# Softmax attention on one core: the maxima products read every fourth query as strided weights

## The reference

```python
B, S, D = 2, 2048, 256          # the input is (2, 2048, 256)
H, DH = 16, 64
q = (c_q @ w_up_q.T).reshape(b, s, H, DH).transpose(0, 2, 1, 3)
k = (c_kv @ w_up_k.T).reshape(b, s, H, DH).transpose(0, 2, 1, 3)
v = (c_kv @ w_up_v.T).reshape(b, s, H, DH).transpose(0, 2, 1, 3)
q = _apply_rope_subspace(q, DR)
k = _apply_rope_subspace(k, DR)
scale = 1.0 / np.sqrt(DH)
scores = jnp.einsum('bhqd,bhkd->bhqk', q, k) * scale
attn = jax.nn.softmax(scores, axis=-1)
out = jnp.einsum('bhqk,bhkd->bhqd', attn, v)
out = out.transpose(0, 2, 1, 3).reshape(b, s, H * DH)
out = out @ w_out.T + residual
```

## Time and profile before

| | us |
|---|---|
| median of 3 runs | 4254.92 (4253.44 to 4257.21) |
| profiled execution | 4258.81 |
| its span, first to last instruction | 4257.0 |
| TensorE, matmuls busy | 3884.0 (91%) |
| TensorE, weight loads busy | 2962.6 (70%) |
| VectorE busy | 3592.9 (84%) |
| ScalarE busy | 2636.8 (62%) |
| GpSimd busy | 2218.4 (52%) |
| granted TensorE clock, mean | 0.952 |

### The profile page before, as it was taken

How to read it: one execution, slowest core, us unless ns; L and a number is a source line. 1 busy time by engine, 2 the same in 40 slices (tenths; PEclk the granted TensorE clock), 3 DMA queues, 4 the chain that set the end, 5 groups by cost and what they waited for, 6 DMA issues and landing times. The chain is left out here.

```text
span 4257.0 us, 54965 instructions
## 1 busy us (share of the span) xinstructions
PE 3884.0 (91%) x17786; PEld 2962.6 (70%) x17786; DVE 3592.9 (84%) x4513; ACT 2636.8 (62%) x3523; POOL 2218.4 (52%) x1841
## 2 busy tenths in 40 slices
PE   7959978869999999999999999999999999989563
PEld 4635535548888888888888888888888888867421
DVE  7845558869999999999999999999999999946521
ACT  6724334347777777777777777777777777732221
POOL 2547756745555555555555555555555555520155
PEclk9969989989999999999999999999999999989676
DMA  7223446842232222332222322224222232046295
GB/s 267 53 60 61 67 105 241 271 128 54 52 77 59 57 56 50 69 69 55 57 51 60 79 53 61 52 52 84 52 59 54 52 74 62 17 152 220 64 250 111
DMA packets 323409, 379.73 MB, mean 89 GB/s; under 512 B 141388, under 2 KB 250769, under 8 KB 310067
## 3 DMA queue, kind: packets, MB, share of 16 engines
q1 hardware_dynamic: 298486, 345.70, 32.2%
q0 software_dynamic: 24640, 30.52, 4.2%
HBM read 232.47 MB, written 117.79 MB: 82 GB/s over the span
## 5 line engine op out<-in xcount | busy, mean ns | idle before, releaser
L1592 POOL TENSOR_TENSOR at_pl<-at_pf,at_ph 128x512 fp32r<-128x512 f32 x1024 | 1328.8, 1298 | 1314.0 <-ACT at_ph L1739 1313.9
L1738 ACT ACTIVATE at_pf<-at_ps_s 128x1024 f32<-128x1024 f32 x1024 | 1051.5, 1027 | 728.2 <-PE at_ps_s L1791 728.2
L1655 DVE TENSOR_TENSOR at_pl<-at_pf,at_ph 128x512 fp32r<-128x512 f32 x1024 | 1349.3, 1318 | 22.3 <-ACT at_ph L1739 22.3
L1637 DVE TENSOR_REDUCE at_mx<-at_ps_u 128x2 f32<-128x1024 f32 x1016 | 1240.1, 1221 | 12.8 <-PE at_ps_u L1775 9.2
L1739 ACT ACTIVATE at_ph<-at_ps_s 128x1024 fp32r<-128x1024 f32 x1024 | 1044.6, 1020 | 0.0
L1807 PE MATMUL at_ps_v<-at_ph,at_vh 128*128 128x512 f32 x2048 | 810.7, 396 | 0.2 <-POOL at_pl L1592 0.2
L1809 PE MATMUL at_ps_v<-at_pl,at_vh 128*128 128x512 f32 x2048 | 808.9, 395 | 0.0
L1808 PE MATMUL at_ps_v<-at_ph,at_vl 128*128 128x512 f32 x2048 | 806.9, 394 | 0.0
L1808 PEld LDWEIGHTS at_ps_v<-at_ph,at_vl 128*128 128x128 f32 x2048 | 388.2, 190 | 91.5
L1807 PEld LDWEIGHTS at_ps_v<-at_ph,at_vh 128*128 128x128 f32 x2048 | 387.4, 189 | 92.3 <-POOL at_pl L1592 0.6
L1809 PEld LDWEIGHTS at_ps_v<-at_pl,at_vh 128*128 128x128 f32 x2048 | 384.9, 188 | 90.2
(11 more groups left out here) (274 smaller groups left out, 4910.3 us busy)
## 6 DMA issues: line engine op xcount, KB each, us to landing
wgu<-Wgu_in SPq DMA_DIRECT2D x64, 384.0 KB, 5.1
qT<-pj_rot SPq DMA_DIRECT2D x32, 512.0 KB, 5.5
vT<-pj_vo SPq DMA_DIRECT2D x16, 1024.0 KB, 5.8
kT<-pj_rot SPq DMA_DIRECT2D x32, 512.0 KB, 3.1
k<-kT SPq DMA_DIRECT2D x32, 512.0 KB, 10.4
q<-qT SPq DMA_DIRECT2D x32, 512.0 KB, 9.4
at_q<-at_low SPq DMA_DIRECT2D x128, 128.0 KB, 2.3
at_vf<-vT SPq DMA_DIRECT2D x32, 512.0 KB, 8.6
```

What stands on the lines that cost most here:

```text
L1592: pool.tensor_tensor(pl[:, n % NP, at], pf[:, n % NP, at], ph[:, n % NP, at].bitcast(F32), ALU.subtract).then_inc(s["pl2_ready"], 1)
L1637: dve.tensor_reduce(mx[:, qb % 2, 2 * i:2 * i + 2], maxima_at(base, j)[:, 0:2], X, ALU.max).then_inc(s["u_max"], 1)
L1655: dve.tensor_tensor(pl[:, n % NP, at], pf[:, n % NP, at], ph[:, n % NP, at].bitcast(F32), ALU.subtract)\
L1738: act.activation(pf[:, n % NP], ps_s[:, n % 2], ACT.Exp, scale=DH ** -0.5)
```

## The change

The tile `qp`, the semaphore `qp_ready`, the function `gather_queries` with its calls and the wait of `products` are removed. The weights of a maxima product are read from `q1` itself, with a step of four elements (16 bytes) between the 128 columns. Both matmuls of a product read them so. Nothing else is changed.

```diff
--- before.py
+++ after.py
@@ -1423,7 +1423,6 @@
             k2 = [self.k2_0, sb("k2_1", [P, L], F32R)]
             q1 = [self.q1_0, sb("q1_1", [P, L], F32R)]
             q2 = [sb(f"q2_{i}", [P, L], F32R) for i in range(2)]
-            qp = sb("qp", [P, L], F32R)
             raw = [self.raw0, sb("raw_1", [P, L], F32R)]
             cut = sb("cut", [P, 2, QB], U32)
             low = sb("low", [P, 2, QB], F32R)
@@ -1445,7 +1444,7 @@
             ps_s = ps("ps_s", [P, 2, 2 * QB])
             ps_v = ps("ps_v", [P, 2, QB])
             ps_u = ps("ps_u", [P, 2, QB])
-            names = ("turns raw0 raw1 kq0 kq1 v0 v1 fixed own cut_ready low_ready low0 low1 qp_ready u_full u_max mg_ready nm_ready "
+            names = ("turns raw0 raw1 kq0 kq1 v0 v1 fixed own cut_ready low_ready low0 low1 u_full u_max mg_ready nm_ready "
                      "row0 row1 row2 row3 s_full p_ready pl_ready pl2_ready vh_ready v_split pv_done "
                      "o_ready o0_out o1_out den recip rden").split()
             s = {n: sem(n) for n in names}
@@ -1720,35 +1719,19 @@
                     act.wait_ge(s[f"o{qb % 2}_out"], g * 64 + (32 * (qb // 2) + 32))
                     act.activation(o_st[:, qb % 2], ps_v[0:DH + 1, qb % 2], ACT.Copy).then_inc(s["o_ready"], 1)
 
-                def gather_queries(g, hh, half, qb):
-
-                    if qb == 0:
-                        loaded(act, "kq", hh, half, 64)
-                    if not isinstance(g, int) or g > 0:
-                        act.wait_ge(s["u_full"], g * SLOTS + ((qb + 1) * PER - SLOTS))
-                    at = slice(qb * QB, (qb + 1) * QB)
-                    act.activation(qp[:, at].rearrange("d (t p) -> d t p", t=NQB),
-                                   q1[hh][:, at].bitcast(F32).rearrange("d (p t) -> d t p", t=NQB), ACT.Copy)\
-                        .then_inc(s["qp_ready"], 1)
-
-                def pair(pr, last=False):
+                def pair(pr):
                     for n in range(2 * SLOTS):
                         act.wait_ge(s["s_full"], pr * (2 * SLOTS) + (n + 1))
                         act.wait_ge(s["pv_done"], pr * (2 * SLOTS) + (n + 1))
                         act.activation(pf[:, n % NP], ps_s[:, n % 2], ACT.Exp, scale=DH ** -0.5)
                         act.activation(ph[:, n % NP], ps_s[:, n % 2], ACT.Exp, scale=DH ** -0.5)\
                             .then_inc(s["p_ready"], 1)
-                        if n % PER == PER - 2 and not (last and n >= SLOTS):
-                            hh, qb = n // SLOTS, n % SLOTS // PER
-                            gather_queries(pr * 2 + (hh + 1), 1 - hh, pr + hh, qb)
                         if n % PER == 2 and n > PER:
                             output(pr * 2 + (n - PER) // SLOTS, (n - PER) % SLOTS // PER)
                         elif n == 2 and pr > 0:
                             output(pr * 2 - 1, NQB - 1)
-                for qb in range(NQB):
-                    gather_queries(0, 0, 0, qb)
                 for pr in range(PAIRS):
-                    pair(pr, pr == PAIRS - 1)
+                    pair(pr)
                 output(HEADS - 1, NQB - 1)
 
             @block.tensor
@@ -1767,9 +1750,7 @@
                             pe.wait_ge(s["u_max"], j - 2)
                     else:
                         pe.wait_ge(s["u_max"], base * SLOTS + j)
-                    if i == 0:
-                        pe.wait_ge(s["qp_ready"], base * NQB + qb + 1)
-                    tile = qp[:, qb * QB + i // 2 * P:qb * QB + (i // 2 + 1) * P]
+                    tile = q1[hh][:, qb * QB:(qb + 1) * QB].rearrange("d (p t) -> d t p", t=NQB)[:, i // 2]
                     for w in range(2):
                         kb = i % 2 * 2 + w
                         m = pe.matmul(maxima_at(base, j)[:, w], tile, k1[hh][:, kb * QB:(kb + 1) * QB],
```

## The result

| | before | changed |
|---|---|---|
| median, us | 4257.52 (6 runs, 4253.44 to 4265.77) | 4274.26 (6 runs, 4269.42 to 4277.09) |
| ratio | | 1.0037, 95% interval 1.0024 to 1.0050 |

The account below looks back on a forecast made before the run. TensorE was taken as the bound. Gathers, waits, start, loads (to +6) and addresses (-6 to +6) at 0 us each left 4255 us on the median's scale; the stated range was 4238 to 4390.

Parts of the forecast that it names:

- TensorE is the bound and waits for nobody: Stretch from 900 to 3700 us: TensorE busy 2794 of 2800 us, its matmuls starting 0.23 us apart without waiting.
- Gathers 0, their wait 0: ScalarE's 128 gathers, 143.5 us, and the products' wait on qp_ready: removing them gives 0 us.
- The length of the strided load: Weight load of a maxima product: 106 ns contiguous, estimated at 106, 150, 235 or 237 strided, against 234 of cover.
- VectorE's row (150): Load estimate from VectorE's reduction of 64 bf16 with a 32-byte step: 0.34 ns more an element, 150 ns a load.
- Addresses 0, -6 to +6: Buffers behind qp move by 8 KB a partition: 0 us expected, -6 to +6 possible over 1024 slots.
- Loads 0, to +6: 2048 strided loads of the products, taken as covered by the matmul ahead: 0 us, at most 3 ns each, +6 us.
- the forecast's own part of the range: Whole kernel without the rivals: 4255 us on the median's scale, 4246 to 4267, chance 53%.
- Rival A: Products' strided load outlasts its 234 ns cover: +172 us (4427) at three times the contiguous load, +389 at four; 18%.
- Rival B: Strided load in time, but its reads hold up the matmul beside it: 60 ns each, +123 us, 4378; 17%.
- What would show it: Signs in the trace after: matmul starts 0.234 us apart; forecast falls if a slot exceeds 2.81 or is under 2.78 us.
- the sign of the matmul count: TensorE's stretch from 900 to 3700 us: 11972 matmuls, give or take 25, if the forecast is right.
- the sign of C: Shorter slots, also in operations not reading q1, would show relief for TensorE: at most -41 us, 4214; chance 12%.

Follow-up runs that it names:

- flat_pad: Changed kernel with an unused 8 KB tile where qp stood, contiguous weight loads from q1 and the exponent's scale a sixteenth; ratio 0.9999, loop 2854.7 us.
- shift: Kernel before, gather and contiguous loads kept, with qp allocated behind all other buffers of the stage; ratio 0.9993, loop 2852.3 us.
- pad: Changed kernel with an unused tile of 8 KB a partition where qp stood, so buffers keep their old addresses; ratio 1.0027, loop 2867.9 us.
- cols96: Changed kernel, addresses as before, with strided loads of 96 instead of 128 columns and the exponent's scale a sixteenth; ratio 1.0045, loop 2873.8 us.
- bench3: Kernel before plus rows of 48 matmuls of 512 columns ahead of the attention, loads of 32 to 128 columns; starts 226.6 to 246.0 ns apart.

## Why the prediction was right in part, and where it was wrong

- *TensorE is the bound and waits for nobody*: right. The loop's +14.3 us are the whole change, with no wait in it.
- *Gathers 0, their wait 0*: right, -0.1 us in flat_pad. The 143.5 us of ScalarE's time came back as its waiting for TensorE.
- *The length of the strided load*: right. From ScalarE's gather by ratio 235 ns were estimated, 234 were measured; VectorE's row (150) was the wrong neighbour. TensorE's load pays nearly ScalarE's factor for this step, 2.1 against the 2.2 worked out there. That the match is so close is in part luck: the contiguous load took 112 ns by itself and not 106.
- *Addresses 0, -6 to +6*: right, -2.5 in shift and +1.2 between pad and the changed kernel.
- *Loads 0, to +6*: wrong, and this is the step that failed: "the ends below the cover leave the time as it is". A load that is in time isn't free. Each costs 6.4 ns, most of it in the distances between the matmuls beside it, 13.1 us in all; that is twice the +6 us at the upper end of the term. The median of 4274 lies above the forecast's own part of the range (up to 4267). It lies in the stated range (4238 to 4390) only because that was widened for the rivals.
- *Rival A*, the load outlasts its cover: not what makes the cost at step 4, since shortening the load to 96 columns keeps four fifths of it. At 128 columns the load is at the edge, so a small part may be A's; step 8 shows it past the edge.
- *Rival B*, the strided load is in time but holds up the matmul beside it: that a covered load costs is what cols96 shows, at the places that B named. That it is the reads which are in the way isn't shown. Its size was off by nine times: 60 ns a load were forecast, 6.4 measured. The mis-sized term is its premise that the 20 ns by which fp32r matmuls stay behind fp32 ones are the load's reads. The bench speaks against that: contiguous loads of 32 columns leave the distance at 231.7 ns, those of 128 at 226.6.
- *What would show it*: the sign named for a fall was a slot over 2.81 us or under 2.78. The median slot came out at 2.809, just inside, and the mean of all, with a few lengthened ones in it, at 2.812, just outside, while the sign of the matmul count, 11972 give or take 25, was clearly broken by 11923. The count was the better one. ScalarE's busy time, forecast at 2493, came out at 2523, for the overlap named above. Shorter slots, the sign of C, didn't come.

What stays open: what a strided load that is in time does to the stream, by its reads or by its length, and why the distances in the bench move by 7 ns with contiguous loads of different lengths and fall to 226.6 at 32 strided columns. The Trainium skill (TensorE: Matmul & The Clock Gate, "Step-by-step: what each phase is for") says that loading the next weights takes no read bandwidth from the running matmul. For contiguous loads no run here speaks against it (32 columns are no faster than 128). A strided load does delay the matmuls, by some 5 ns at 96 columns (9.7 for two in cols96, 5.5 in bench3); whether read bandwidth is what it takes, no run here shows.

## What to carry to other kernels

Where TensorE runs without a gap, work taken from an engine that waits for it is worth nothing, and the trade must be judged by what it adds to TensorE, down to single ns: 6.4 ns on 2048 loads were 13 us. A weight load whose own time fits into its cover may still slow the matmuls, so a strided stationary operand (the weights) wants a price of its own, taken from a run with the same step and a shorter load, beside the question whether it is covered. If a stride can't be avoided for fp32, a step of two lengthened the load by 5 ns and this kernel's loop not at all, and one of four or more doubled the load. A row of matmuls by themselves is a poor measure of a few ns: step 2 stood 6.8 ns above step 1 there and cost nothing in the kernel.

## What the runs showed of the hardware

- A weight load of 128 fp32 columns takes 0.112 us at step 1, 0.117 at step 2, 0.175 at step 3, 0.234 at step 4 and 0.239 at step 8. At step 4 it takes the same at 1.2 and at 2.4 GHz (0.233 and 0.234).
- In bench3 fp32r matmuls of 512 columns come every 226.6 to 246.0 ns, (11.95 - 0.39)/47 for step 8 being the last, with no engine waiting and at a granted clock of 1.00; the distance changes with the length and the step of the load beside them. In some rows it is the same from start to start (226 or 227 ns at step 1 with 128 columns and at step 4 with 32; 233 or 234 at step 2 with 128 and at step 4 with 64), in the others it goes to and fro between 224 and 252.
- In cols96, where VectorE's reductions go over 96 instead of 128 partitions, the halves of the same subtraction took 1035 ns on VectorE and 1765 on GpSimd, against 1312 and 1298 in the changed kernel. Why is open.
